# Values and state in one TensorE product: a linear attention block with an FFN on one core

## The reference

```
q, k, v = split(LN(x) @ W_attn + b_attn)       # 16 heads of 32
q, k    = elu(q) + 1, elu(k) + 1               # per head
kv_t    = kv_(t-1) + k_t (outer) v_t ;  ksum_t = ksum_(t-1) + k_t
y_t     = (q_t . kv_t) / (q_t . ksum_t + 1e-6) # causal, the state starts at 0 for each of the 8 sequences
x       = x + y @ W_proj + b_proj
x       = x + fp8(LN(x)) @ fp8(weight).T + bias
```

## Time and profile before

| | us |
|---|---|
| median of three runs | 1013.76 |
| profiled execution | 1014.31 |
| its span, first to last instruction | 1012.6 |
| TensorE busy | 982.0 |
| VectorE busy | 701.7 |
| GpSimd busy | 535.3 |
| ScalarE busy | 463.6 |

### The profile page before, as it was taken

One profiled execution on the slowest core, in us unless ns is written; L12 is line 12 of the kernel. 1 busy time (PEld: TensorE's weight loads), 2 busy tenths in 40 slices (PEclk: granted clock), 3 DMA queues, 4 the chain that ended last, 5 costly groups with the idle time before them and its releaser, 6 DMA issues.

```text
span 1012.6 us, 43583 instructions
## 1 busy us (share of the span) xinstructions
PE 982.0 (97%) x19504; PEld 549.5 (54%) x19504; DVE 701.7 (69%) x1448; ACT 463.6 (46%) x714; POOL 535.3 (53%) x523
## 2 busy tenths in 40 slices
PE   5999999999999999999999999999999999999895
PEld 2454555555555555555555555555555555555552
DVE  6888677677767677676767767767776767754573
ACT  5753452544545364453535445254454535445222
POOL 3545675564565565465456456456456556533323
PEclk9999999999999999999999999999999999999997
DMA  8714334333334334334342244343332543322211
GB/s 271 113 35 80 94 76 81 86 77 84 80 75 91 75 75 94 72 83 88 71 96 74 71 93 79 78 88 75 83 83 75 90 77 75 81 44 54 55 35 48
DMA packets 185355, 82.51 MB, mean 81 GB/s; under 512 B 165840, under 2 KB 165840, under 8 KB 185168
## 3 DMA queue, kind: packets, MB, share of 16 engines
q1 hardware_dynamic: 185168, 79.73, 34.9%
HBM read 22.81 MB, written 16.78 MB: 39 GB/s over the span
## 4 chain that ended last, share of the span: by engine, by line
PE 91%; DVE 3%; POOL 2%; ACT 1%; issue 1%; DMA 0%; ACTq 0%; POOLq 0%
PE R L231 74%; PE S L231 15%; PE R L235 3%; POOL st L875 1%; DVE st L606 1%; DVE xs L696 0%; POOL xn L877 0%; POOL x L877 0%; DVE raw L800 0%; DMA xs<-in_L_attn_x 0%; POOL xs L918 0%; POOL sm L902 0%; DVE qk L629 0%; DVE wpl L778 0%; ACT qk L448 0%
## 5 line engine op out<-in xcount | busy, mean ns | idle before, releaser
L231 PE MATMUL R<-xt,wh 128*128 128x512 f16 x1024 | 306.2, 381 | 2.4 <-ACT wh L439 2.4
L629 DVE SCALAR_TENSOR_TENSOR qk<-qk,rel 128x512 f32<-128x512 f32 x128 | 141.3, 1105 | 151.1 <-ACT rel L451 151.1
L909 POOL TENSOR_TENSOR yhl<-y,yhl 128x512 f16<-128x512 f32 x60 | 69.9, 1165 | 311.2 <-ACT yhl L439 311.2
L231 PE MATMUL R<-xt,wl 128*128 128x512 f16 x512 | 194.4, 381 | 0.0
L875 POOL TENSOR_TENSOR st<-st,half 128x1 f32<-128x1 f32 x128 | 94.8, 741 | 138.3 <-DVE st L611 125.4
L231 PE MATMUL R<-wh,xt 128*128 128x512 f16 x512 | 160.3, 379 | 0.0
L231 PEld LDWEIGHTS R<-xt,wh 128*128 128x128 f16 x1024 | 96.7, 98 | 108.4 <-DVE xt L744 2.6
L231 PE MATMUL R<-wph,yt 128*128 128x512 f16 x512 | 134.6, 386 | 2.8 <-DVE yt L689 2.8
L439 ACT ACTIVATE yhl<-y 128x512 f16<-128x512 f32 x60 | 37.8, 630 | 209.5 <-DVE y L683 209.5
L448 ACT ACTIVATE qk<-R,bqk,wm 128x512 f32<-128x512 f32 x128 | 98.9, 772 | 54.0 <-PE R L231 54.0
L897 POOL TENSOR_TENSOR xs<-xs,bp 128x512 f32<-128x512 f32 x64 | 110.4, 1731 | 0.1
(11 more groups left out here) (91 smaller groups left out, 1498.0 us busy)
## 6 DMA issues: line engine op xcount, KB each, us to landing
xs<-in_L_attn_x SPq DMA_DIRECT2D x64, 256.0 KB, 3.8
out<-xs SPq DMA_DIRECT2D x64, 256.0 KB, 2.4
raw<-in_L_attn_W_attn SPq DMA_DIRECT2D x3, 1024.0 KB, 9.6
xs<-in_L_attn_W_proj SPq DMA_DIRECT2D x4, 256.0 KB
raw<-in_L_ffn_weight SPq DMA_DIRECT2D x1, 1024.0 KB, 16.2
x2t<-x2b SPq DMA_TRANSPOSE x62, 2.3
xt<-xnhl SPq DMA_TRANSPOSE x60, 3.1
yt<-yhl SPq DMA_TRANSPOSE x60, 3.2
```

The costliest lines, as they stand in the source:

```text
L231: return e.matmul(out, a, b, start=start, stop=stop, skip_group_check=True)
L629: e.scalar_tensor_tensor(qk[j % 2][:, i, :], qk[j % 2][:, i, :], 1.0, rel[:, (u - 1) % 2, :], ALU.min, ALU.add).then_inc(s_phi, 1)
L909: e.tensor_tensor(yhl[:, n % 2, 1, :], y[:, :], yhl[:, n % 2, 0, :], ALU.subtract).then_inc(s_yl, 1)
```

## The change

One product of 128 rows takes the place of two sums. For half a of a tile, 64 of the 128 rows hold the masked scores against v of that half, and the other 64 hold q against the state. Two heads share those 64 rows: q of h and of its neighbour stand there, and in the other operand the state of head h stands in its own 32 rows, with zeros in the 32 rows of its neighbour.

- `v1` becomes a ring of `NV` = 5 tiles, with two parts (a) for each. The zeros are written once, at the start, by a GpSimd memset of 5280 elements for each partition, and the ones by two affine selects. `v_out` writes each half by itself (two VectorE instructions in place of one). `sm` lies where a weight was staged.
- `queries` (ScalarE) copies q into `sm`, 4 instructions of 64 partitions x 512. It waits for the values before (`s_av`).
- `spread` (ScalarE) copies state and mid into `v1`, 8 instructions of 32 partitions x 132. `values` waits for it.
- `values` has 64 calls, in pieces of 32 queries: 128 rows and 32 columns each. `from_state` is gone.
- The mask is all VectorE's: 2 instructions of 64 partitions x 1024. ScalarE's copy of the scores and GpSimd's mask are gone. The division writes y in one instruction in place of three.
- `update(n+1)` stands behind `ffn(n-2)` and ahead of `scores(n+1)` on TensorE, and behind `proj` on VectorE. On VectorE `scores(n)` stands ahead of the statistics.
- The low part of x is GpSimd's, and its high part stands behind ktok on ScalarE.
- At a sequence's first tile the state is set to zero and read like any other.
- Two of the four sums of the FFN weight (`ffn_sum`) stand right behind the mask of tile 1, the other two behind `update(2)`.

```diff
 (TensorE)
-            def from_state(n):
...
             def values(n):
                 src, v, j, c = parts(n)
+                pe.wait_ge(s_smd, n + 1)
+                pe.wait_ge(s_q, n + 1)
+                pe.wait_ge(s_v, n + 1)
+                pe.wait_ge(s_spread, n + 1)
                 for g in range(4):
+                    for h in range(4):
+                        for i in range(4):
+                            a, b = divmod(i, 2)
+                            at = g * HALF + 32 * b
+                            mm = matmul(Y[32 * i:32 * i + 32, h, g * W:(g + 1) * W], sm[:, h, a, at:at + 32],
+                                        v[:, a, 4 * g + h, :], True, True)
                 mm.then_inc(s_av, 1)
...
                 if n >= 2:
                     t2(n - 2)
                     ffn(n - 2)
+                if n + 1 < NT:
+                    update(n + 1)
 (ScalarE)
+            def queries(n):
...
+                for a in range(2):
+                    for p in range(2):
+                        q = src[half_rows(p), 0:4, tokens(n, a)[0]].unsqueeze(1).broadcast_to([HALF, 2, 4, HALF])
+                        dst = sm[half_rows(1 - a), 2 * p:2 * p + 2, a, :].rearrange("p h (g t) -> p h g t", g=4)
+                        made = copy(dst, q)
+                made.then_inc(s_q, 1)
+            def spread(n):
...
+                for a in range(2):
+                    act.wait_ge(*((s_mid, n + 1) if a else (s_state, n + 1)))
+                    held = mid if a else state[:, n % 2, :]
+                    for h in range(4):
+                        at, rows = HALF * (1 - a) + 32 * (h % 2), slice(32 * h, 32 * h + 32)
+                        made = copy(v[at:at + 32, a, :, h, :], held[rows, :].rearrange("p (g w) -> p g w", g=4))
+                made.then_inc(s_spread, 1)
 (ScalarE, loop)
                     if n + 1 < NT:
                         k_tokens(n + 1)
+                    if n + 8 < NT:
+                        ln1_parts(n + 8)
                     if n:
                         ahead(chunks(n)[1])
+                    if n + 1 < NT:
+                        queries(n + 1)
                     values(n)
...
                 if n >= 2:
                     ffn(n - 2)
+                if n + 1 < NT:
+                    spread(n + 1)
 (VectorE)
             def scores(n):
+                for a in range(2):
+                    dst = sm[half_rows(a), :, a, :].rearrange("p h (g t) -> p h g t", g=4)
+                    made = e.tensor_tensor(dst, scored(a), causal_over(a), ALU.mult)
+                made.then_inc(s_smd, 1)
```

More of the change, by code:

```diff
@@ L323, in scores @@
                             rows = slice(32 * h, 32 * h + 32)
-                            matmul(S[out, h, g * HALF:(g + 1) * HALF], src[rows, 4 + g, cols], src[rows, g, cols], True, True)
-            def from_state(n):
[L328 to L342, removed]
+                            mm = matmul(S[out, h, g * HALF:(g + 1) * HALF], src[rows, 4 + g, cols], src[rows, g, cols],
+                                        True, True)
@@ L344, in values @@
+                mm.then_inc(s_score, 1)
             def values(n):
                 src, v, j, c = parts(n)
[L346 to L349 removed]
+                pe.wait_ge(s_smd, n + 1)
+                pe.wait_ge(s_q, n + 1)
                 pe.wait_ge(s_v, n + 1)
[L351 to L357 removed]
+                pe.wait_ge(s_spread, n + 1)
@@ L575, in _ @@
                 if n < NT:
-                    scores(n)
                     if n == 0:
+                        spread(n)
                         proj_weight()
@@ L634, in v_out @@
                 dve.wait_ge(s_bv, 1)
[L635 to L646 removed]
+                n = 4 * j + t
@@ new lines, in v_out @@
+                dve.wait_ge(s_one, 2)
+                if n >= NV:
+                    dve.wait_ge(s_av, n - NV + 1)
+                for a in range(2):
+                    rows = half_rows(a)
+                    made = e.scalar_tensor_tensor(v1[rows, n % NV, a, :, 0:32], heads(bank["qkv", j, 8 + t][rows, :]),
+                                                  UN_V[rows], heads(bv[rows, :]), ALU.mult, ALU.add)
+                made.then_inc(s_v, 1)
+            def scores(n):
+                dve.wait_ge(s_score, n + 1)
+                dve.wait_ge(s_causal, 3)
+                if n:
+                    dve.wait_ge(s_av, n)
+                for a in range(2):
+                    dst = sm[half_rows(a), :, a, :].rearrange("p h (g t) -> p h g t", g=4)
+                    made = e.tensor_tensor(dst, scored(a), causal_over(a), ALU.mult)
+                made.then_inc(s_smd, 1)
@@ L658, in update @@
                 if n % PER < PER - 1:
                     dve.wait_ge(s_mid, n + 1)
-                    e.tensor_tensor(new, bank["delta", n, 1][:, 0:4 * W], mid[:, :], ALU.add).then_inc(s_state, 1)
+                    e.tensor_tensor(state[:, (n + 1) % 2, :], bank["delta", n, 1][:, 0:4 * W], mid[:, :],
+                                    ALU.add).then_inc(s_state, 1)
+                elif n + 1 < NT:
+                    e.memset(state[:, (n + 1) % 2, :], 0.0).then_inc(s_state, 1)
             def values(n):
@@ L795, in ffn_round, with ffn_sum @@
                                 saturate=False).then_inc(s_wfd, 1)
-            def ffn_sum():
+            def ffn_sum(first, end):
                 dve.wait_ge(s_wfd, 3)
-                for f in range(4):
+                for f in range(first, end):
                     e.tensor_tensor(w_b[:, f, :], w_hi[:, f, :], w_lo[:, f, :], ALU.add).then_inc(s_wfd, 1)
+            no_state()
             for m in range(4):
@@ L897, in add_bp @@
                 e.tensor_tensor(x, x, bp[:, :], ALU.add).then_inc(s_xb, 1)
-            def scores(n):
-                if not alone(n):
-                    pool.wait_ge(s_scopy, n)
-                    e.tensor_tensor(sm[:, 2:4, :, :], sm[:, 2:4, :, :], causal_over(2), ALU.mult).then_inc(s_sel, 1)
             def values(n):
@@ L924, in _ @@
             e.memset(half[:, :], -0.5).then_inc(s_half, 1)
-            for i in range(2):
-                e.memset(v1[i][:, :, :, 32:33], 1.0).then_inc(s_one, 1)
             for m in range(4):
```

141 lines of the change are left out of this document (56 added, 85 removed).

## The result

The changed kernel takes 988.82 us, the median of four runs (987.15 to 989.57); the kernel before took 1013.48 beside it (1012.71 to 1015.6). The ratio is 0.9751, with a 95% interval of 0.9731 to 0.9771. The profiled execution took 989.57 us, its span is 987.8. The forecast was 993.0.

A forecast was written before the change was run, and what follows sets the result against it. The prediction took TensorE's issued work to bound the kernel: 1014.3 - 39.0 (from_state) + 19.2 (values) + 0.5 (memset) - 2.0 (mask waits) = 993.0 us. The 8-in-10 range was 977 to 1020 us.

The forecast's parts named there:

- What bounds it: TensorE, busy for 847.83 of 848.00 us in the middle, sets the time; a tile is a closed cycle of 15.10 us.
- from_state goes: On TensorE the from_state products vanish: 0.63 us a tile, 0.46 in a sequence's first tile, 39.0 us in all.
- Values doubles: On TensorE values grows from 64 to 128 pairs, from 0.92 to 1.22 us a tile, adding 19.2 us.
- my two bounds: For the 128 pairs of values on TensorE: 1.12 us at update's pace, 1.32 at that of scores and from_state.
- Rival A: On TensorE the 128 pairs of values take 1.53 us or more; 1033 us at 1.84, 1060 at 2.25; chance 0.18.
- Rival B: On TensorE weight loading alone sets the pace of values, 0.92 us for 128 pairs, 974 us in all; chance 0.10.
- The order: On TensorE, update moved between FFN and scores costs 0, between -0.15 and +0.15 us a tile, with five form changes as before.
- ScalarE and VectorE: Their changed work stays hidden behind TensorE at cost 0: ScalarE 12.9 us in a three-feature tile, VectorE about 10.3 to 11.4.
- rival D: ScalarE becomes the bound in tiles with three features, half of the tiles lose their gain, 1004 us; chance 0.10.
- The ends: At start and tail: GpSimd's memset +0.5 us, TensorE's waits for GpSimd's mask gone -2.0, the last tile 0.
- The sum: All terms applied to the profiled execution of 1014.3 us give 993.0 us; likeliest case's own range 984 to 1002.

The follow-up runs named there:

- the repeated run: The changed kernel run once more with no edit, beside the kernel before: 988.89 us, ratio 0.9758.
- the run piece by piece: The changed kernel with the loop over the four pieces of queries outermost in values, 32 pairs in a row to each piece: 1144.64 us in one run.

## Why the prediction was right, step by step

**What bounds it.** Right. The time is what TensorE issues: 0.41 us a tile over 41 tiles, as its timeline says, TensorE is busy for 822.98 of 823.00 us in the repeated run, and spread made twice on ScalarE costs the middle 2.9 us in all.

**from_state goes, 39.0 us.** Right: 0.63 us in a tile.

**Values doubles, +19.2 us.** The mechanism was right, the term too large: it took 1.10 us from first to last start, not 1.22, so 64 x 0.18 = 11.5 us. The lower of my two bounds (1.12, update's pace) was the true one: what sets the pace is 8.6 ns a pair of small instructions, the same with four pieces as with eight. Rival A (1.53 or more) was in the right place with its argument: with 64 columns it is 1.84 us and the change makes the kernel 1.7% slower. The 32 columns decide it. Rival B (0.92) is what the pieces alone would allow, 0.94 by the run piece by piece; the pace of issue stops it at 1.10.

**The order, 0.** This step gave the right number for the wrong reason, and it is the one that failed. I counted forms and waits, and found the position of update free between -0.15 and +0.15 us a tile. It costs nothing in the changed kernel. But "free" is false: with values grown to 128 pairs, update right behind it makes 192 small pairs in a row, and TensorE stops within them every second to fifth tile, which with the clock behind the stops made some 59 of 62 us. What the step lacked was the number of TensorE's instructions in a row, and with it, as far as the traces tell, the time until the next ones are there. The change of values and the move of update are thus one change. In the kernel before no run of small pairs was longer than 128 (values and update, or scores and from_state), and it stalled once, in update(60). The changed kernel has runs of 128 too, values by itself and update with scores, and it too stalls once (this is the timeline in tile 60):

```profile
931.21 1.36 PE L219 MATMUL S<-v,raw 128*32 128x33 f32 x120
934.46 0.27 PE L219 MATMUL S<-v,raw 128*32 128x33 f32 x8 [1.89 <-issue]
```

In that tile the pieces ahead are few and the small runs follow each other within 9.7 us in place of 14.6.

**ScalarE and VectorE, 0.** The durations were right: queries 628 ns for 630, spread 314 for 315, the mask 1218 for 1200; ScalarE busy for 743.6 us where 751 was forecast. No wait came once a tile, so rival D did not happen. But the parts of x were not worth 0: left where they were they cost 8.8 us. That is no price of the change, it is one that its move avoided, and I had not asked what would have happened without it.

**The ends, -1.5 us.** Wrong by 4.2. The sum of the terms as measured is -39.0 + 11.5 = -27.5, and the span fell by 24.8, so the ends cost 2.7 (0.9 of it in the 41 middle tiles, which gave 16.7 us where the terms give 17.6). The memset took 4.5 us, for the forecast's 4, and values(0) started 1.0 earlier. I took the waits for GpSimd's mask as gone and did not put the new ones in: the wait for y(1) at 82 us, and the mask in the last two tiles. There the mask has no pieces as cover, and stands behind the second norm and ffn on VectorE:

```profile
961.91 0.91 PE L219 MATMUL S<-qk 32*64 32x64 f32 x64
...
962.83 0.69 DVE L697 TENSOR_TENSOR xs<-o,xs 128x512 f32<-128x512 f16 x1
...
963.45 2.45 DVE L641 TENSOR_TENSOR raw<-S,causal 64x1024 f32<-64x1024 f32 x2
...
965.95 1.99 PE L219 MATMUL S<-v,raw 128*32 128x33 f32 x128 [2.54 <-DVE raw L641]
```

From scores to the end of values it is 6.03 us (961.91 to 965.95 + 1.99), where I had 4.84 and the earlier trace rows give 4.37. 0.6 of the 1.2 missed are the mask's late start behind L697, 0.6 are values, 1.99 us in place of the 1.44 that I counted: the granted clock is 0.50 there, at the 1.2 GHz level. In the repeated run values(62), behind a like wait of 2.1 us, took 1.43 at a clock of 1.00, and values(63) 1.99 at 0.50. In the last tile it is given back: y of the tile before is transposed while TensorE waits, proj(62) follows values(63) at once, where it waited 1.4 us for that transpose in the kernel before, and from values(63) to the end it is 2.6 us less.

**The sum.** 993.0 forecast, 989.6 in the profiled execution: 7.7 better by values, 4.2 worse by the ends.

## What to carry to other kernels

Where TensorE is full, a chain of small products may be packed by rows as long as its column pieces stay narrow: price it with the pace of one piece (57 ns a pair for 64 columns, 29 for 32, divided by the pieces side by side) and with the pace of issue (8.6 ns a pair), and take the larger. Then count how many such pairs stand in a row once the work is regrouped, and put large products between the runs: an order that is free at 128 may cost 6% at 192. Each change of form that this adds costs 0.10 us. A masked or copied operand that is hidden in the middle needs to be looked at again in the first and last tiles, where nothing covers it, and an early value put ahead of others on an engine that works in order holds all of them.

## What the runs showed of the hardware

- 192 small pairs in a row (384 instructions of TensorE in some 2 us) make it stop for 1.9 to 2.9 us, every second to fifth tile; the intervals are often the same number of products, 636, 890 or 1526. The view of waits shows no releaser. 128 pairs in a row do so only once in the whole run. At each of the 18 stops a transfer of 16 KB on the instruction queue starts 2.2 to 3.0 us before the next product, and the intervals are 5, 7 and 12 times the 255 instructions that TensorE has for each such transfer. That it waits for them is argued, not shown by a run of its own.
- After such a stop of 2 us the granted clock fell in 11 of 18 cases to 0.66 to 0.68 over the next 5 us, and stayed at 1.00 in 7.
- A pair of small float32 products goes at 8.6 ns on four pieces of 128 rows, 8.8 on eight pieces of 64 rows. A single piece takes 29.4 ns for a pair with 32 weight columns, 57.5 with 64.
- One more change of array form in a tile (update between proj and ffn) costs 0.10 us.
- Instructions of the same shape are faster on both engines in the changed kernel: VectorE's feature fell from 1105 to 768 ns on the mean, GpSimd's bias from 1731 to 1284. That VectorE's low part of x went is not the reason: in the run that put it back the two were 744 and 1328, and the low part itself took 1208 ns, for 1576 before. Scores' copy and GpSimd's mask are gone in both; no run changed the mask alone.
